# A graph attention loop with a longer gather ring, earlier index loads, weights in PSUM and a reordered VectorE chain

## The reference, cut to what matters

```
# layer 0: graph attention, 8 heads of 32
h  = (x @ W).reshape(n, 8, 32)
a1, a2 = sum(h * attn_l, -1), sum(h * attn_r, -1)
e  = leaky_relu(a1[src] + a2[dst], 0.2)
ex = exp(e - segment_max(e, dst)[dst])
alpha = ex / segment_sum(ex, dst)[dst]
out = segment_sum(h[src] * alpha[:, :, None], dst)
# layer 1: relational graph network, 16 relations
seg = dst * 16 + edge_type
agg = segment_sum(x[src], seg) / max(segment_sum(1, seg), 1)
out = einsum(agg.reshape(n, 16, 256), weight) + x @ root
```

## Time and profile before

| | us |
|---|---|
| median of 3 runs | 9834.04 |
| lowest, highest | 9813.71, 9865.91 |
| the profiled execution | 9886.75 |
| its span, first to last instruction | 9884.9 |

### The profile page before, as it was taken

One profiled execution on the slowest core, in us unless ns is written; L12 is line 12 of the kernel. 1 busy time (PEld: TensorE's weight loads), 2 busy tenths in 40 slices (PEclk: granted clock), 3 DMA queues, 4 the chain that ended last, 5 costly groups with the idle time before them and its releaser, 6 DMA issues. The chain is left out here.

```text
span 9884.9 us, 142531 instructions
## 1 busy us (share of the span) xinstructions
PE 6513.6 (66%) x35938; PEld 4877.4 (49%) x35939; DVE 3983.1 (40%) x10933; ACT 2039.3 (21%) x4033; POOL 3826.3 (39%) x3655
## 2 busy tenths in 40 slices
PE   2584565656666566557919999566666766776675
PEld 2463444444444444445604444455666665665553
DVE  3311565655665565562351111433333333333433
ACT  0363221222222222223402222100000000100121
POOL 0001555555555545503110000355555555555233
PEclk9865777777777777758959999777777777777688
DMA  4001222222222222222212222122222222222234
GB/s 130 18 0 54 69 71 68 70 66 75 72 70 70 75 65 73 73 80 98 90 42 106 106 102 104 43 71 70 73 72 72 77 72 70 77 76 70 56 120 122
DMA packets 396509, 738.39 MB, mean 75 GB/s; under 512 B 143870, under 2 KB 263968, under 8 KB 383136
## 3 DMA queue, kind: packets, MB, share of 16 engines
q0 software_dynamic: 174720, 490.64, 17.8%
q1 hardware_dynamic: 221728, 247.11, 7.4%
HBM read 558.25 MB, written 193.82 MB: 76 GB/s over the span
## 5 line engine op out<-in xcount | busy, mean ns | idle before, releaser
L789 POOL DMA_INDIRECT ga_ring<-h_dram,ga_idx x1624 | 1814.9, 1118 | 2382.9 <-DMA ga_starts<-start_dram 1900.2
L789 POOL DMA_INDIRECT rg_ring<-y_dram,rg_idx x1624 | 1627.9, 1002 | 2552.0 <-DMA rg_idx<-src_rel 2071.8
L1110 PE MATMUL ga_psS<-ga_msg,ga_hot_f 128*128 128x280 f32 x4032 | 1359.5, 500 | 226.4 <-DVE ga_msg L1147 139.2
L1328 PE MATMUL rg_psS<-rg_ring,rg_onehot 128*128 x4032 | 1159.6, 449 | 321.3 <-DVE xb L1367 237.8
L1110 PEld LDWEIGHTS ga_psS<-ga_msg,ga_hot_f 128*128 128x128 f32 x4032 | 960.3, 245 | 551.1 <-issue 285.5
L1328 PEld LDWEIGHTS rg_psS<-rg_ring,rg_onehot 128*128 128x128 f32 x4032 | 900.9, 229 | 491.2 <-issue 340.9
L1296 ACT COPY rg_onehot_t<-rg_psT 128x512 f32<-128x512 f32 x508 | 272.7, 589 | 2695.1 <-DMA f_x<-xg_dram 1249.2
L1101 PE MATMUL ga_psL<-ga_look,ga_hot_t 128*128 x6072 | 251.2, 171 | 732.3 <-DVE ga_look L1220 385.2
L1310 PE MATMUL rg_psT<-ident,rg_onehot 128*128 128x128 f32 x2032 | 338.5, 321 | 568.5 <-DVE rg_onehot L864 322.6
L1493 PE MATMUL rr_psY<-rr_wr,rr_xt 128*128 128x512 f32 x1568 | 686.0, 595 | 0.0
L1318 PE MATMUL rg_psL<-icnt,rg_onehot_t 128*128 x4048 | 625.7, 297 | 49.6 <-issue 49.3
(11 more groups left out here) (312 smaller groups left out, 8803.8 us busy)
## 6 DMA issues: line engine op xcount, KB each, us to landing
y_dram<-rr_y SPq DMA_DIRECT2D x98, 1024.0 KB
f_x<-xg_dram SPq DMA_DIRECT2D x224, 128.0 KB
yg_dram<-f_y SPq DMA_DIRECT2D x224, 128.0 KB
ga_starts<-start_dram SPq DMA_DIRECT2D x1624, 4.0 KB
ga_ring<-h_dram,ga_idx POOLq DMA_INDIRECT x1624
rg_ring<-y_dram,rg_idx POOLq DMA_INDIRECT x1624
xg_dram<-x SPq DMA_DIRECT2D x2, 6272.0 KB
f_w<-L_ffn_W SPq DMA_DIRECT2D x16, 512.0 KB
```

The source lines that it names most:

```text
L789: p.indirect_dma_start(ring[:, s * G + j, :], None, table, bass.IndirectOffsetOnAxis(ap=idx[:, s, j:j + 1], axis=0)).then_inc(gathered[s], 16)
L1110: o = pe.matmul(psS[:, u % 2, 0:MROW], hot_f[:, u % 2, j, :], msg[:, u % 2, j, :], start=j == 0, stop=j == G - 1)
L1328: o = pe.matmul(psS[:, 0:C], onehot[:, u, j, :], ring[:, ds((g % R) * G + j, 1), :], start=j == 0, stop=j == G - 1)
```

## The change

- R goes from 6 to 8 groups; `idx` and `starts` get 2R = 16 slots of their own, and the loads of group g + 5 are issued when group g has landed. Before a gather POOL waits for its indices and for `room`; SP gives `room` when the last pair on the slot's old group is done. SP, not POOL, reports a landed group. Both loops use this.
- `start_dram` holds the flags eight times over, once per head, group by group, so one DMA of 64 rows loads a group's flags where eight of 8 rows did. `setup` writes it by 16 DMAs of rows of 4 KB.
- The weights `w` of the attention loop stand in PSUM (`psW`). `psQ` moves into the bank of `psI`.
- A new block `count_up` writes the node numbers to PSUM once (`psN`, bf16). `mark` becomes a small subtraction (`distance`) and one `tensor_tensor` with a bf16 output of 1024 numbers per partition. The one-hots are now stored node by node, so PE and ACT read one column of edges with a step of 16 bytes.
- DVE's step is written in another order, with six drains; `old` and one copy go. PE turns the one-hots ahead of the maxima and splits `sum_up` in halves around `turn_runs`; ACT's `power` goes ahead of `stage`.

The chain of the maxima moved up behind the messages, and the one-hots (one instruction, L1217) stand near the end of the step. The diff, cut:

```diff
-R = 6
+R = 8
+EARLY = 3
@@ setup
-                sp.dma_start(k.start_dram.rearrange("(r p) n -> p r n", p=P),
-                             starts[:].rearrange("p (r n) -> p r n", n=P)).then_inc(tab2, 16)
+                for r in range(z.ROWS):
+                    lo, hi = r * P, min((r + 1) * P, z.NGT)
+                    for h in range(HEADS):
+                        sp.dma_start(k.start_dram[lo:hi, h, :, :].rearrange("g j n -> g (j n)"),
+                                     starts[0:hi - lo, r * GE:(r + 1) * GE]).then_inc(tab2, 16)
@@ gather_groups, SP
+        def report(s, visit):
+            sp.wait_ge(gathered[s], visit * 16 * G)
+            sp.sem_inc(ready, 1)
+        def make_room(g):
+            pair = sp.value_load(k.last_pair[0:1, ds(g - R, 1)], min_val=1, max_val=z.T)
             sp.wait_ge(freed, done(pair - 1))
-            load(i * R + s, s)
+            sp.sem_inc(room, 1)
+        def turn(i, q, fetch=True, follow=True):
+            report(q % R, i * 2 + (q // R + 1))
+            if follow:
+                make_room(i * R2 + (q + 2))
+            if fetch:
+                load(i * R2 + (q + 2 + EARLY), (q + 2 + EARLY) % R2)
@@ gather_groups, POOL
+            if not (isinstance(i, int) and i * R2 + q < R):
+                p.wait_ge(room, i * R2 + (q + 1 - R))
             p.sem_inc(go, 1)
-        def report(i, s):
-            p.wait_ge(gathered[s], (i + 1) * 16 * G)
-            p.sem_inc(ready, 1)
@@ attend
-        hot_b = sb("hot_b", [P, U, G, P], BF16)
+        hot_b = sb("hot_b", [P, U, P, G], BF16)
-        w = sb("w", [P, U, G + 1, HEADS])
+        w = psW[:, 0:U * (G + 1) * HEADS].rearrange("p (u j h) -> p u j h", u=U, j=G + 1)
-                    act.copy(hot_f[:, u % 2, :, :], hot_b[:, u % U, :, :]).then_inc(hot_wide, 1)
+                    act.copy(hot_f[:, u % 2, :, :], hot_b[:, u % U, :, :].rearrange("p n j -> p j n")).then_inc(hot_wide, 1)
-                        o = pe.transpose(psT[:, j, :], hot_b[:, u % U, j, :], k.ident_b[:])
+                        o = pe.transpose(psT[:, j, :], hot_b[:, u % U, :, j], k.ident_b[:])
-                            o = pe.matmul(psX_v[:, j, :], hot_b[:, u % U, j, :], runs[:, u % 2, q, j, :],
+                            o = pe.matmul(psX_v[:, j, :], hot_b[:, u % U, :, j], runs[:, u % 2, q, j, :],
+                def distance(t, u, g):
+                    v.tensor_scalar(near[:, u % 2, :], k.dstf[:, ds(g * G, G)], k.pair_node[:, ds(t, 1)], None,
+                                    ALU.subtract)
-                    for j in range(G):
-                        o = v.tensor_scalar(hot_b[:, u % U, j, :], k.iota_b[:], k.pair_node[:, ds(t, 1)],
-                                            k.dstf[:, ds(g * G + j, 1)], ALU.add, ALU.is_equal)
-                    o.then_inc(hot, 1)
+                    v.tensor_tensor(hot_b[:, u % U, :, :], psN[:],
+                                    near[:, u % 2, :].unsqueeze(1).to_broadcast([P, P, G]), ALU.is_equal
+                                    ).then_inc(hot, 1)
```

More of the change, by code:

```diff
@@ L750, in _, with gather_groups @@
                 project(NB - 1, (NB - 1) % 2)
[L753 to L758, removed]
+def gather_groups(nc, z, block, k, table, rows, ring, idx, landed, gathered, ready, room, go, freed, starts=None):
+    per = 32 if starts is not None else 16
+    R2 = 2 * R
     @block.sync
@@ L764, in load @@
             if starts is not None:
[L765 to L771, removed]
-            sp.wait_ge(freed, done(pair - 1))
-            load(i * R + s, s)
[L774 to L778, removed]
@@ new lines, in turn @@
+        def turn(i, q, fetch=True, follow=True):
[4 more added lines that the diff above has]
+                load(i * R2 + (q + 2 + EARLY), (q + 2 + EARLY) % R2)
+        for g in range(R + EARLY):
+            load(g, g)
+        for g in range(R - 2):
+            report(g, 1)
+        for q in range(R - 2, R2):
+            turn(0, q)
+        n = (z.NGT - 2 - EARLY) // R2
+        with sp.Fori(1, n) as i:
+            for q in range(R2):
+                turn(i, q)
@@ L811, in _ @@
-        report((z.NGT - 1) // R, (z.NGT - 1) % R)
+                p.indirect_dma_start(ring[:, (q % R) * G + j, :], None, table,
+                                     bass.IndirectOffsetOnAxis(ap=idx[:, q, j:j + 1], axis=0)
+                                     ).then_inc(gathered[q % R], 16)
+        for q in range(R2):
+            gather(0, q)
+        with p.Fori(1, z.NGT // R2) as i:
+            for q in range(R2):
+                gather(i, q)
+        for g in range(z.NGT // R2 * R2, z.NGT):
+            gather(g // R2, g % R2)
@@ L1186, in rest, with step @@
                                     ).then_inc(run, 1)
-                def logs(t, u, g, b, early):
+                def step(t, u, group, block_no):
+                    early = isinstance(t, int)
+                    now, before = not early or t >= 0, not early or t >= 1
+                    n1, n2, n3, n4 = (not early or t + q >= 0 for q in (1, 2, 3, 4))
+                    b = block_no(2)
                     own = high_f[:, ds(b * HEADS, HEADS)]
@@ new lines, in step @@
+                    if n1:
+                        g = group(1)
+                        v.wait_ge(looked, done(t + 1))
+                        v.tensor_tensor(esum[:], ring[:, ds(slot(g), G), HC1:HROW], psL_v[:, :, 0:HEADS], ALU.add)
+                    if n2:
+                        v.wait_ge(maxed, done(t + 2))
+                        v.tensor_reduce(red[:], psX_v.rearrange("p j h -> p h j"), AX.X, ALU.max)
+                    if before:
+                        fade(t - 1, u - 1, block_no(-1))
@@ new lines, in step @@
+                    if n2:
+                        v.scalar_tensor_tensor(log[:], tot[:], SLOPE, tot[:], ALU.mult, ALU.max)
+                    if n4:
+                        distance(t + 4, u + 4, group(4))
+                    if n1:
+                        relate(t + 1, u + 1, group(1))
+                    v.drain()
+                    if n2:
+                        v.tensor_tensor(new[:], log[:], own, ALU.max)
+                        v.tensor_tensor(first, log[:], own, ALU.max)
+                    if before:
+                        add_up(t - 1, u - 1, block_no(-1))
```

185 lines of the change are left out of this document (95 added, 90 removed).

## The result

| | before | after |
|---|---|---|
| median, us | 9823.88 (4 runs) | 10127.47 (4 runs) |
| lowest, highest | 9812.59, 9865.91 | 10108.7, 10182.48 |
| span of the profiled run | 9884.9 | 10180.0 |
| attention loop, mean step | 13.03 | 14.33 |
| relation loop, mean step | 11.73 | 11.46 |

The ratio is 1.031, 95% interval 1.0258 to 1.0363. The forecast was 9070 in a range of 8200 to 9800.

What follows compares the result with a forecast made beforehand. POOL accounts for both loops, its gathering and the other engines' work alternating in phases that add up. From 9834: -240 - (822 - 274) + 24 = -764, giving 9070 us; 8-in-10 range 8200 to 9800.

Steps and rivals of the forecast that it cites:

- Weights in PSUM: Attention loop: gathers no longer held up by DVE's messages, mean 1118 to 970 ns, 240 us saved, between 0 and 279.
- What is given back: Both loops: more gathers beside the work, where others crawl, return a third, 274 of 822 us; ends nothing and all.
- Loads ahead: POOL's load waits shrink to 0.5 us for room: 466 us saved in the attention loop, 218 in the relation loop.
- The report on SP and the ring: SP's landing reports cost nothing; the ring of 8 gives nothing, between -1 and +1% of the two loops (63 us).
- One-hots and chain: DVE's attention step: one-hot operation 1.2 us, fewer drains; step 9.06 to 8.3 us (7.6 at lowest), worth 138 us.
- Strided loads: PE's one-hot reads with a 16-byte step: 0.035 us each taken, 24 a step; ACT's widening covered.
- rival D: Attention loop: strided loads at 0.25 us make PE the bound, 10278 us; decides from 0.135 us a load; chance 0.12.
- PSUM for DVE: DVE reading weights from PSUM costs nothing a row shows; the skill's 60 versus 125 ns would add 24 us.
- Rival C: Both loops: work and gathers exclude each other, saved waits given back whole, only gather price gains: 9618 us; chance 0.22.
- Rival B: Both loops: the crawl goes away with the small loads or POOL's reports, POOL sets the pace: 7738 us; chance 0.13.
- Once only: Setup: flags written eight times over cost 18 us and count_up 6, together +24 us.

Runs made afterwards that it cites:

- e1: The changed kernel with a ring of 7 groups in place of 8; 10173.97 us, ratio 1.025 to the kernel before, first kind of chip.
- e2: The changed kernel with a ring of 7 and the weights w back in SBUF; 9696.92 us, ratio 0.979 to the kernel before, first kind of chip.
- e17: The kernel before with only the new gathering (ring of 7), its step and SBUF weights kept; 9730.19 us, ratio 0.979, first kind of chip.
- e10: The kernel before with the changed step, keeping the gathering of before (ring of 6); 7844.32 us, ratio 0.962, second kind of chip.
- e12: The changed kernel with a ring of 7 and weights in SBUF, on the second kind of chip; 8091.71 us, ratio 0.993 to the kernel before.

## Why the prediction was wrong, point by point

- **Weights in PSUM**: the term was sized well (970 ns forecast, 949 measured; 240 us forecast, 274 measured) and had the wrong sign. I took the 3.02 us gather for a cost. On the first kind of chip it was also what cut POOL's stream at the messages, once in 9 us, and beside a stream that isn't cut PE slows after 6 to 8 us. The term that was left out is what e1 minus e2 measures, 477 us net of the gather's gain.
- **What is given back** was the failing step: "The ends are nothing and all." By the forecast's own sum (-240 - 822 + 24 with nothing given back) the measured +304 asks for some 1340 us given back, where "all" was 822: the new overlap of gathers and work didn't only fail to pay, it made the work slower. The sizing was weak before that. "A good third" doesn't follow from its numbers: 2302 and 2283 are together 1226 more than 3359, over half of either. The trace had two windows that said how PE fares while POOL doesn't pause, 4.35 of 25 us, and what I asked of them was only how much of the gain they would eat. I did not ask what ends such a phase or what keeps it from starting. A gap in POOL's stream was to be seen there, the lock of the earlier trace rows. The stretch from 2010 holds two (3.02 us at 2011.30, 2.51 at 2020.88), and PE keeps its pace there but for a gap of 1.3 us before 2022.40; it slows at 2031.4, behind seven gathers of 0.95 with no gap but the issue. Then the trace goes on:

```profile
2032.44 1.96 POOL L789 DMA_INDIRECT ga_ring<-h_dram,ga_idx  x1 [0.30 <-issue]
2032.88 0.17 PE L1101 MATMUL ga_psL<-ga_look,ga_hot_t 128*128 x1 [1.49 <-issue]
...
2033.60 0.17 PE L1101 MATMUL ga_psL<-ga_look,ga_hot_t 128*128 x1 [0.55 <-issue]
...
2034.33 0.17 PE L1101 MATMUL ga_psL<-ga_look,ga_hot_t 128*128 x1 [0.55 <-issue]
```

  The messages at 2031.24 held this gather by only 1.0 us, against 2.1 and 1.6 us before, and PE stayed slow until the gathers ended. So the lock protects PE in part, as far as its gaps are long enough and in time.
- **Loads ahead**: the waits for loads are gone, and POOL starts 0.84 us behind the messages (2026.99 to 2027.83), where I estimated 0.5. Alone it gains 2.1% on the first kind (e17), 220 us of the 684 that I put down before anything was given back; on the second, nothing, since POOL had few waits to lose.
- **The report on SP and the ring**: cost nothing that shows, as forecast; e1 and the whole change have 1.025 and 1.031, with overlapping intervals.
- **One-hots and chain**: better than forecast. The one operation takes 684 ns, not 1200, and the free step is 7.47 us, below even the 7.6 of my lower end. None of it shows in the total on the first kind: with weights in SBUF, the whole change (e2) and the new gathering alone (e17) have the same ratio, 0.979.
- **Strided loads, rival D**: its time, 10278, is near the measured one, by another mechanism. The maxima went from 0.56 to 1.08 us, 0.033 us a load and not the 0.135 from which D decides; the turns from 0.61 to 0.71. ACT's widening doubled, 1045 to 2116 ns, under cover: it is busy 957 of 3500 us. Here the rule of the Trainium skill (SBUF — State Buffer, SBUF: two separate sides, Door 1: The DMA port swizzle) that each new 16-byte line has its price agrees with the measurement in kind; the price is small.
- **PSUM for DVE**: the messages take 2357 ns (median) with `w` in PSUM (e1) and 2358 with `w` in SBUF (e2). The 65 ns an operation of the Trainium skill (Perfetto Trace Analysis, Optimizing Scalar/DVE Operations) aren't there.
- **Rival C** named the right relation, work and gathers that exclude each other, and took "given back whole" for the worst. **Rival B** has the pace of the second kind of chip, forecast 7738, measured 7862, but not its reason: nothing that the change removes ended the slow phases, they are absent there with the small loads and POOL's reports in place, too (e10). Nothing in the trace of before could tell that such chips exist.
- **Once only**: +24 forecast. POOL's first gather starts at 934.9 in place of 917.2, 18 us, and the first messages 36 us later.

**Still open**: what connects POOL's gathers and PE on the first kind of chip. The runs show that the stream must be unbroken for some 6 us, that a pause of 2.7 us mends it, and that halving the bytes doesn't; not why matmuls then stand 0.7 us apart, nor how the chips differ. Halving the bytes left the number of gathers and of rows as it was, so those in flight aren't told apart from POOL's issuing as such. The halved bytes were tried in the relation loop alone, where PE's signals come late but few of its starts stand 0.7 us apart. "Kind of chip" is read from the time of the kernel before on at least five chips; none was seen to change its kind, but a condition of the machine around them would look the same.

## What to carry to other kernels

Before a lock, a wait or a slow operation is taken away from an engine that feeds the others, look at what the others do when it runs without a break, in a trace in which it does. A pause that looks like waste may be what paces it, and then the gain has to come with another pace (here a wait for the landing after each fourth gather, 1.5% faster than before in place of 3% slower, or the lock itself together with earlier loads, 2.1% faster). And measure on more than one chip: the same change was 1.031 on one and 0.964 on another; the changed kernel with its weights in SBUF (e2, e12) is the one whose ratio was below 1 on both, 0.979 and 0.993.

## What the runs showed of the hardware that was not expected

- Two kinds of chips, 9810 to 9950 and 8152 to 8157 us for one kernel. On the first, PE slows in the attention loop beside POOL's unbroken gathers to a start each 0.7 us or a multiple of it, and its signals reach the others late, some only when the gathers have ended (18 us late in the stretch shown, 12 us in the one of the relation loop); on the second neither happens.
- A DVE operation with both inputs in SBUF held up a gather that started beside it for up to 2 us; with one of them in PSUM it didn't (means of 1097 and 946 ns, e2 and e1).
- A bf16 comparison of 1024 elements per partition from PSUM took 684 ns, where a float32 product of 1024 took 1225.
- A weight load of bf16 with a step of 16 bytes cost 0.033 us more than one in a piece (16 of them with their products, 0.56 and 1.08 us), and ACT's copy of 1024 elements with it 1.07 us more.
